# In-place trees of contiguous additions and maxima in place of VectorE's strided reductions in a windowed attention

## The reference

```python
q = _pointwise(Wq, bq, x); k = _pointwise(Wk, bk, cond); v = _pointwise(Wv, bv, cond)
k = jnp.pad(k, ((0, 0), (0, 0), (pad_left, pad_right)))      # 8 left, 7 right
v = jnp.pad(v, ((0, 0), (0, 0), (pad_left, pad_right)))
idx = jnp.arange(T)[:, None] + jnp.arange(W)[None, :]        # W = 16 neighbours
k_win = k[:, :, idx].reshape(B, H, hd, T, W)                 # H = 8 heads of hd = 8
v_win = v[:, :, idx].reshape(B, H, hd, T, W)
dots = jnp.einsum('bhdt,bhdtw->bhtw', qh, k_win) * scale
attn = jax.nn.softmax(dots, axis=-1)
out = jnp.einsum('bhtw,bhdtw->bhdt', attn, v_win)
return _pointwise(Wo, bo, out.reshape(B, C, T))
```

## Time and profile before

| What | Value |
|---|---|
| Median of the runs | 1786.49 us (1783.93 to 1788.33) |
| Span of the profiled execution | 1795.9 us |
| Scores, first group (until the first maximum) | 69.1 to 211.2 us |
| Maxima, outputs, first group | 211.2 to 367.7 us |
| Scores, second group | 367.7 to 478.8 us |
| Maxima, outputs, second group | 478.8 to 619.5 us |
| VectorE busy over the span | 1070.0 us (60%) |
| GpSimd busy over the span | 460.4 us (26%) |
| TensorE matmul busy over the span | 1372.4 us (76%) |

### The profile page before, as it was taken

How to read it: one execution, slowest core, us unless ns; L and a number is a source line. 1 busy time by engine, 2 the same in 40 slices (tenths; PEclk the granted TensorE clock), 3 DMA queues, 4 the chain that set the end, 5 groups by cost and what they waited for, 6 DMA issues and landing times. The chain is left out here.

```text
span 1795.9 us, 16524 instructions
## 1 busy us (share of the span) xinstructions
PE 1372.4 (76%) x4645; PEld 785.6 (44%) x4646; DVE 1070.0 (60%) x1635; ACT 420.6 (23%) x1173; POOL 460.4 (26%) x150
## 2 busy tenths in 40 slices
PE   5257477564078568999899989998999698889970
PEld 2023156321066245555455545554555343267740
DVE  3499999999999976157325722572257354112224
ACT  3011110000010133244224422432233210024430
POOL 1454199963099100000000000000000004132325
PEclk9678788878588789999999999999999899589995
DMA  6711140030000260000010001000000360145547
GB/s 221 219 47 70 58 94 0 0 140 0 0 0 1 69 236 1 9 15 1 1 23 0 0 0 23 0 0 0 0 0 0 139 278 1 48 125 167 165 140 245
DMA packets 62148, 114.06 MB, mean 64 GB/s; under 512 B 22305, under 2 KB 26881, under 8 KB 61330
## 3 DMA queue, kind: packets, MB, share of 16 engines
q1 hardware_dynamic: 47186, 69.43, 12.0%
q0 software_dynamic: 7424, 21.00, 4.3%
q10 hardware_dynamic: 7488, 23.07, 3.3%
HBM read 75.68 MB, written 37.79 MB: 63 GB/s over the span
## 5 line engine op out<-in xcount | busy, mean ns | idle before, releaser
L922 POOL DMA_INDIRECT table<-ids,slot_of x32 | 30.8, 964 | 918.8 <-DVE slot_of L1149 909.4
L242 POOL TENSOR_TENSOR gprod<-dots,v_h 128x4096 f32<-128x4096 f32 x16 | 188.7, 11828 | 115.6 <-ACT dots L282 115.6
L233 POOL TENSOR_TENSOR gprod<-q_h,k_h 128x4096 f32<-128x4096 f32 x16 | 155.0, 9700 | 121.4 <-DMA k_h<-by_row 61.4
L697 PE MATMUL big_ps<-wo_sb,ot 128*128 128x512 f32 x384 | 176.2, 594 | 7.6 <-DVE ot L811 7.6
L318 PE MATMUL sum_ps<-gprod,ident 128*128 128x512 f32 x256 | 121.6, 631 | 69.7 <-POOL gprod L233 49.4
L688 PE MATMUL big_ps<-ht,wq_sb 128*128 128x512 f32 x384 | 171.4, 592 | 0.0
L332 PE MATMUL sum_ps<-gprod,ident 128*128 128x256 f32 x512 | 130.2, 419 | 43.9 <-POOL gprod L242 43.9
L654 ACT ACTIVATE probs<-s_ps,npeak 128x128 f32<-128x128 f32 x256 | 91.6, 362 | 270.1 <-PE p_ps L744 233.2
L332 PEld LDWEIGHTS sum_ps<-gprod,ident 128*128 128x128 f32 x512 | 107.6, 212 | 65.9 <-issue 48.6
L373 DVE TENSOR_TENSOR prod<-q_h,k_h 128x4096 f32<-128x4096 f32 x16 | 110.7, 6920 | 31.6 <-DMA k_h<-by_row 29.8
L398 DVE TENSOR_REDUCE o_h<-prod 128x256 f32<-128x4096 f32 x16 | 116.4, 7274 | 0.6
(11 more groups left out here) (189 smaller groups left out, 2188.1 us busy)
## 6 DMA issues: line engine op xcount, KB each, us to landing
wr<-in_w_routed ACTq DMA_DIRECT2D x4, 3072.0 KB, 21.4
y_rows<-y_sb SPq DMA_DIRECT2D x48, 256.0 KB, 2.0
by_row<-stage ACTq DMA_DIRECT2D x8, 768.0 KB, 3.8
X<-in_x SPq DMA_DIRECT2D x4, 1024.0 KB, 9.2
cond<-in_ctx SPq DMA_DIRECT2D x16, 256.0 KB, 2.6
by_row<-stage ACTq DMA_DIRECT2D x8, 512.0 KB, 3.2
q_h<-by_row SPq DMA_DIRECT2D x4, 1024.0 KB, 8.0
k_h<-by_row SPq DMA_DIRECT2D x4, 1024.0 KB, 12.6
```

The source lines that it names most:

```text
L233: nc.gpsimd.tensor_tensor(gprod[:, s], q_h[:, :, :], k_h[:, :, bass.ds(4 * i + (2 * s + 1), DIM)], ALU.mult).then_inc(multiplied, 1)
L242: nc.gpsimd.tensor_tensor(by_window(gprod[:, s]), half_of(dots, half), window(d, half), ALU.mult).then_inc(multiplied, 1)
L697: last = nc.tensor.matmul(ps[:, :], ot[:, a % 2, c, k * P:(k + 1) * P], wo_sb[:, a * HC + c, :], start=(c == 0), stop=(c == HC - 1))
```

## The change

VectorE's three reductions are each replaced by a tree of `tensor_tensor` instructions that halve the number of terms in place: for the scores 8 terms to 4, 2 and 1 (2048, 1024 and 512 elements), for the outputs and for the maxima 16 terms to 8, 4, 2 and 1 (2048, 1024, 512 and 256 elements). Each of these waits for the one ahead of it. The maxima use `prod` as scratch, so that `dots` stays whole for the subtraction. GpSimd's, TensorE's and ScalarE's programs and all DMAs stay as they are.

```diff
-                    own.enter(i, 4)
+                    own.enter(i, 8)
...
-                        own.done(nc.vector.tensor_reduce(dots[:, 4 * i + 2 * s, :], prod[:].rearrange("p d t -> p t d"),
-                                                         AX_X, ALU.add))
+                        own.done(nc.vector.tensor_tensor(prod[:, 0:4, :], prod[:, 0:4, :], prod[:, 4:8, :], ALU.add))
+                        own.done(nc.vector.tensor_tensor(prod[:, 0:2, :], prod[:, 0:2, :], prod[:, 2:4, :], ALU.add))
+                        own.done(nc.vector.tensor_tensor(dots[:, 4 * i + 2 * s, :], prod[:, 0, :], prod[:, 1, :], ALU.add))
...
-                    own.done(nc.vector.tensor_reduce(half_of(peak, half), half_of(dots, half).rearrange("p w t -> p t w"),
-                                                     AX_X, ALU.max))
+                    highest = prod[:].rearrange("p a b -> p (a b)").rearrange("p (w t) -> p w t", w=WINDOW)
+                    own.done(nc.vector.tensor_tensor(highest[:, 0:8, :], half_of(dots[:, 0:8, :], half),
+                                                     half_of(dots[:, 8:16, :], half), ALU.max))
+                    for n in (4, 2):
+                        own.done(nc.vector.tensor_tensor(highest[:, 0:n, :], highest[:, 0:n, :], highest[:, n:2 * n, :], ALU.max))
+                    own.done(nc.vector.tensor_tensor(half_of(peak, half), highest[:, 0, :], highest[:, 1, :], ALU.max))
...
-                        own.done(nc.vector.tensor_reduce(half_of(o_h[:, d, :], half),
-                                                         by_window(prod).rearrange("p w t -> p t w"), AX_X, ALU.add))
+                        terms = by_window(prod)
+                        for n in (8, 4, 2):
+                            own.done(nc.vector.tensor_tensor(terms[:, 0:n, :], terms[:, 0:n, :], terms[:, n:2 * n, :], ALU.add))
+                        own.done(nc.vector.tensor_tensor(half_of(o_h[:, d, :], half), terms[:, 0, :], terms[:, 1, :], ALU.add))
```

## The result

The changed kernel takes 1834.18 us (median of four runs, 1827.15 to 1838.97) against 1785.27: a ratio of 1.029, 95% interval 1.024 to 1.035. It is slower by 49 us; 60 had been forecast, and a range of 1820 to 1882. Run again beside the last experiments it took 1832.31 against 1780.12, 1.031 (1.026 to 1.037).

A forecast was written before the change was run, and what follows sets the result against it. VectorE was taken to bound the first attention, its two-input instructions and GpSimd's products excluding each other. Trees save 86.6 us, expose 144 and add 2.7 of waiting: +60, so 1846 us, range 1820 to 1882.

The forecast's parts named there:

- The exclusion: First attention: a two-input VectorE instruction and a GpSimd product exclude each other, whole instruction by whole instruction; reductions run free.
- Rivals 1 and 2: GpSimd's products beside the trees: all stay hidden, 1700 us (5%), or half stay hidden, 1773 us (5%).
- The turns: First attention: VectorE's two-input instructions and GpSimd's products take turns; about 3 us of gaps remain at 32 turns.
- Rival 3: GpSimd starves in the attention: its products come only when VectorE has run out of work; 1882 us, 6%.
- What is newly exposed: GpSimd's 255 us of products, less 108 already paid and about 3 of gaps: 144 us lose the reductions' cover.
- the sum: Whole kernel: -86.6 + 144 + 2.7 = +60 us, giving 1846 us.
- What VectorE saves: Trees save 41.8 us in the scores, 44.8 in outputs and maxima; 86.6 together if nothing holds VectorE up.
- The wait that grows: End of the first group's scores: the maximum waits 3.4 us for the last odd sum, 2.7 more.
- The price of an element in place: Trees with operands in one buffer: nothing extra taken; upper bound the reductions' own 1.71 ns an element.
- Rival 4: In-place trees run at the reductions' rate: no saving, and the cover gone; 1933 us, 2%.
- By stretch: Four stretches of the first attention, scores and outputs of each group: +5 or so, +38, -4, +22 us.
- the maxima: Four maxima as trees in the first attention, each saving 2.24 us, counted within the 44.8 us.

The follow-up runs named there:

- the two versions with cut products: GpSimd's products cut to 64 of 4096 elements: in the changed kernel (trees) 1581.67 us, 0.888; in the kernel before (reductions) 1677.47 us, 0.941.
- the parts: Kernel before with trees only for outputs: 1842.92 us, 1.034; only for scores and maxima: 1790.27, 1.005; only for maxima: 1793.59, 1.007.
- 64 half ones: Changed kernel with each of GpSimd's products cut into two instructions of 2048 elements: 1826.17 us, 1.025.

## Why the prediction was right, point by point

- **The exclusion**: right, and for short instructions too. An addition of 512 elements was held 7.84 us, a maximum of 256 elements 7.83. Rivals 1 and 2 had rested on the doubt about these. The doubt could have been settled beforehand: the prediction says that the trace before shows nothing under 2048 elements beside GpSimd, but there L380, of 512 elements and 0.55 us, was held for 7.1 us at 122.62 (row above). The same row shows that the reduction's one input is not enough of a reason for its going free. In all 32 VectorE instructions of the changed kernel were held for long, one for each product.
- **The turns.** Rival 3 (GpSimd starves) did not come: with 0.03 us between VectorE's steps GpSimd got its turn behind each. It finished the first group's products for outputs at 310.3, when VectorE was in the second of its eight pairs, well ahead as forecast.
- **What is newly exposed**: 255 - 108 - 3 = 144 by the sum; 250 - 103 = 147 by the groups. Right, though not to the 3 us that it seems: both terms are 5 us smaller by the groups, and the 103 is that of one profile (last point).
- **What VectorE saves**: 86.6, less 2.7 for the wait, by the sum; measured 94 in the two profiles, 91 between the two versions with cut products. Too small, in the size of two terms. The gap between two steps in the loop I took as 0.14 us; in the changed kernel's first group it is mostly 0.04, and 0.15 before the last step alone:

```profile
106.86 2.29 DVE L375 TENSOR_TENSOR prod<-prod 128x2048 f32<-128x2048 f32 x1
109.19 1.23 DVE L376 TENSOR_TENSOR prod<-prod 128x1024 f32<-128x1024 f32 x1
110.57 0.69 DVE L377 TENSOR_TENSOR dots<-prod 128x512 f32 x1
...
213.16 2.29 DVE L388 TENSOR_TENSOR prod<-dots 128x2048 f32<-128x2048 f32 x1 [2.76 <-ACT dots L273]
```

  That, with the gap behind the product, is some 3 us over 16 trees. And the reductions that went were longer than the 7.0 I subtracted for the outputs: 7274 ns on average, 4 us over 16. GpSimd is not all of that, since with its products cut they still take 7136 on average, 2 us over 16; what lengthens them is open. With 10 us more saved and 3 more exposed, +60 becomes the measured +53.6.
- **The wait that grows**: 2.76 us, forecast 3.4 (last row above).
- **The price of an element in place**: nothing, as taken; 2048 elements 2.29 us, 1024 elements 1.23, 512 elements 0.69. Rival 4 falls.
- **By stretch**: forecast +5, +38, -4, +22; measured +1.0, +37.6, -7.2, +22.2.
- **A term that was wrong without showing in the total**: the maxima. Nine of the 86.6 us were theirs, as VectorE's work, and that is right; but they don't come off the time in full, since the second half's reduction was cover. Where the outputs stay reductions, the maxima's trees lose 7.2 and 5.4 us, as the parts show. Beside trees for the outputs they gain only 1.7 and 1.5: the stretches are 195.8 and 164.4 us in the version with trees for the outputs only, 194.1 and 162.9 in the whole change.
- **The part that is not settled to the microsecond** is the first group's scores before the change. With the same instructions of all engines up to there they took 142.1 us in the kernel before, 133.2 in the version with trees for the outputs only, 148.4 in the one with trees for the maxima only and 133.2 in the one with trees where GpSimd is still:

```profile
70.00:203.20 133.20, 84.56 (x170) 35.12 (x170) 128.83 (x24) 19.11 (x29) 79.09 (x8) 0.80 0.23 84
```

  Without the time that VectorE stands still there (41.7, 33.6, 48.2 and 33.1 us, counted over all its rows) all four are about 100 us long, so what differs is how much of GpSimd the reductions hide. That this depends on when TensorE hands a buffer back is a guess, not shown. With trees the stretch was 143.1, 142.9 and 144.1 in three profiles. So the +1.0 of that stretch is one draw, which against these four would be anything from -5 to +10, and that the sum fits so well is in part luck. Part of the runs' spread (1762 to 1794 for the kernel before over all jobs) may come from there. It was not tried apart.

## What to carry to other kernels

Before speeding up an instruction, ask what runs under it: here the slow, strided reductions were nearly the only time in which GpSimd's products cost VectorE nothing, and 94 us of VectorE's work saved brought 147 us of waiting. Sum the time of two engines that exclude each other as if they were one, and give GpSimd a two-input product only if it hides or if what it costs there (7.9 us) is less than VectorE's own (4.4). A cheaper form of one step can turn another decision round: once the sums are trees, the products belong on VectorE, and 1725 us is faster than both kernels.

## What the hardware showed that was not expected

- A hold lasts until GpSimd's instruction is over, however short the held one is: 7.83 us for 0.43 us of work. The turns are strict: with trees 32 holds of over 2.5 us for 32 products, and 64 for 64 half ones.
- An instruction with one tensor input can be held as well: L380 took 7.67 us beside GpSimd and 0.55 alone, while a reduction of 4096 elements took 7.23 beside GpSimd and 7.00 without.
- The strided reduction of 4096 elements takes 7.0 us; read in order it takes 4.42, the same as a product. Writing with a step of 8 elements takes 7.52, of 16 elements 7.06.
- GpSimd's product of 4096 elements takes 7.45 us into one half of its buffer and about 8.65 into the other, in the scores; in the outputs 7.9 into both. The two products for the scores also differ in the shift of `k_h` (4i + 1 and 4i + 3). Why is open.
